# Local attention in a six-layer block: the value products with the preceding tile's keys on two row groups of TensorE

## The chip, the cores and the metric

The kernel is one program on one core of a Trainium2 chip. The metric is the device time of one execution in microseconds, as the median of several. The kernel before took 3763.29 us (three runs, 3762.48 to 3780.51).

## The reference, cut to what matters

The input is `x` of shape (8, 512, 128), in float32. A first stage modulates `x` with six vectors made from `c`, and adds one full attention. Then six layers follow, each a local attention with 16 heads of 64 and a gated feed-forward network. All weights are float32. The change touches the local attention alone:

```python
def local_attention(q, k, v):            # (b, h, n, d), windows of w = 32 tokens
    def look(t):                         # a window sees its own and the preceding one
        p = jnp.pad(t, ((0, 0), (0, 0), (1, 0), (0, 0), (0, 0)))
        return jnp.concatenate([p[:, :, :nw], p[:, :, 1:]], axis=3)
    bk2, bv2 = (look(bk), look(bv))
    sim = jnp.einsum('bhwie,bhwje->bhwij', bq, bk2) * QK_SCALE
    sim = jnp.where(mask, -jnp.finfo(sim.dtype).max, sim)
    attn = jax.nn.softmax(sim, -1)
    out = jnp.einsum('bhwij,bhwje->bhwie', attn, bv2)
```

So each window of 32 queries is multiplied with 64 keys and values: the 32 in front of it and its own 32.

## The kernel before, in words

**Tiles.** A sequence of 512 tokens is cut into four tiles of 128 tokens (`TPB` = 4), j = 0 to 3. A tile has four windows. There are 8 sequences and 6 layers, so 192 tiles, numbered n; four tiles of one sequence in one layer are a batch, and there are 48 batches. All activations stay in the core's memory.

**The pipeline.** Each engine runs an order written out by hand, in slots c = 0, 1, 2, ... (`slot`). A slot handles parts of several tiles: the projections of q and k of tile c, the rotary part of tile c-1 on VectorE, the transposes of q and k (`qk_back`) and the scores of tiles c-2 and c-3, softmax of tile c-3, and the value products (`pv`) and output projection (`out_proj`) of tile c-4. The four kinds of slot (c mod 4 = 0 to 3, "slot 0" to "slot 3" below) differ in what the feed-forward network of an earlier batch puts between. As `pv` lags four tiles, the `pv` of tile j stands in slot j. Four slots are called a turn here.

**What happens in a slot.** ScalarE copies projections to `raw` (`to_raw`, L896), squares them (L904), VectorE sums the squares (L1384), GpSimd takes the power -1/2 (`norms`: L1136, then L1138), VectorE multiplies (`normed`, L1390), VectorE and GpSimd each do half of the rotary part (`cos_part` L1398, `sin_part` L1148, both read `raw`), and VectorE adds the two halves (`rotated`, L1404, which does not read `raw`). `to_raw` of tile n writes the half of `raw` that tile n-2 used, and before it waits until `rotated` of tile n-2 is done. ScalarE's order in a slot is: `to_raw` of two pieces, `qk_to_sbuf`, `to_raw`, squares, `to_raw`, the exponentials (L937), `o_to_sbuf` (L943, the copy of the value products, after `pv`), the second squares, the copies of v, and so on. VectorE's order is: sum of squares, row sums of the exponentials, reciprocal, second sum of squares, `probs` (L1362), `probs_back` (L1377, the transpose of the probabilities in 32x32 blocks into `PTd`), `cos_part`, `rotated`, row maxima (L1340), `less_max`, `normed`.

**The moves.** A window's probabilities stand, after `probs_back`, on the window's own 32 partitions, in `PTd`: half 1 for its own keys, half 0 for the 32 keys in front. `bands` on the queue SP moves them to where the product needs them, by 8 transfers of 32 partitions x 2 KB, each with 16 counts on `band_moved`: the own halves to `PT` (L335), the front halves one window up in `PT` (L338), and the front half of window 0 to partitions 96 to 127 of `BT` (L340), since its keys are the last 32 of the tile in front. SP waits for `probs_back` (L1377), and for the `pv` of the tile before, which frees `PT`.

**The product.** `pv` (L620) waits for all eight, and makes 16 matmuls (one per head) with all 128 keys of the tile: stationary 128x64 of `V`, moving 128x128 of `PT`. Heads u = 0 to 3 of each half go to PSUM bank 2, u = 4 to 7 to bank 5; the even and odd heads go to the lower and upper 64 output partitions. For j > 0, 16 more follow (L627) with the 32 keys in front: stationary 32x64 of `V`, moving 32x32 of `BT`, both on partitions 96 to 127. Each float32 matmul is two instructions in the profile, so L627 has 32 per tile, in 144 tiles.

**Around it in slots 2, 3 and 0.** After `pv` of slot 3, TensorE makes two projections, `qk_back` and `out_proj`; ScalarE copies the result (`attn_to_sbuf`, L952); GpSimd adds it to the running sum (`x_between`, L1157), and only then does its `norms` (L1136, L1138) and `ffn_rstd` (L1175, L1177). ScalarE's `ffn_normed` (L980) and TensorE's `norm_back_ffn` (L658) in slot 0 wait for that.

Of the kernel before, what the change touches and what calls it, by code (L numbers as in the profile page):

```python
# [14 lines left out]
HEADS, DH, W = 16, 64, 32  # L15
INNER = HEADS * DH
HID = int(D * 4 * 2 / 3)
P = 128
TPB = S // P
# [5 lines left out]
HH = HEADS // 2  # L25
# [35 lines left out]
def wait(eng, sem, value):  # L61

    if type(value) is int and value <= 0:
        return
    eng.wait_ge(sem, value)


def adaln_block(nc, x_d, wa_d, ba_d, cT_d, wmod_d,
# [3 lines left out]
    with ctx:  # L72
        def sb(name, shape, dt=F32):
            return ctx.enter_context(nc.sbuf_tensor(name, shape, dt))

        def sem(name):
            return ctx.enter_context(nc.semaphore(name))
# [42 lines left out]
        V = sb("V", [P, 2, INNER])  # L120
        mx = sb("mx", [P, HEADS])
        Pr = sb("Pr", [P, 2 * 512])
        PTd = sb("PTd", [P, 2, HEADS, W])
        PT = sb("PT", [P, NWIN, HEADS, W])
        BT = sb("BT", [P, HEADS, W])
        sm = sb("sm", [P, HEADS])
        rs = sb("rs", [P, HEADS])

# [62 lines left out]
        band_moved = sem("band_moved")  # L191
# [46 lines left out]
        v_out = [sem(f"v_out{c}") for c in range(2)]  # L238
# [5 lines left out]
        cos_ready = sem("cos_ready")  # L244
        sin_ready = sem("sin_ready")
        rot_ready = sem("rot_ready")
# [64 lines left out]
        def layer(n):  # L311
            return n // NT

        @block.sync
        def _(sp):

# [12 lines left out]
            def bands(n, j):  # L329

                sp.wait_ge(pT_ready, n + 1)
                wait(sp, pv_done, n)
                for w in range(NWIN):
                    r = slice(w * W, (w + 1) * W)
                    sp.dma_start(PT[r, w, :, :], PTd[r, 1, :, :]).then_inc(band_moved, 16)  # L335
                    if w > 0:
                        before = slice((w - 1) * W, w * W)
                        sp.dma_start(PT[before, w, :, :], PTd[r, 0, :, :]).then_inc(band_moved, 16)  # L338
                    else:
                        sp.dma_start(BT[P - W:P, :, :], PTd[r, 0, :, :]).then_inc(band_moved, 16)  # L340

            def take_x(b, j):

# [5 lines left out]
            def move(l, m):  # L349
                n = l * NT + m  # L350
                if 0 <= n < NI:
                    bands(n, m % TPB)
# [96 lines left out]
        def _(pe):  # L449
# [162 lines left out]

            def pv(n, b, j):

                pe.wait_ge(band_moved, 128 * n + 128)
                pe.wait_ge(v_out[LAST_VO], n + 1)
                for u in range(HH):
                    for h in range(2):
                        hc = (2 * u + h) * DH
                        mm = nc.tensor.matmul(OUT_BANK[u // 4][h * DH:(h + 1) * DH, (u % 4) * P:(u % 4 + 1) * P],  # L620
                                              V[:, j % 2, hc:hc + DH], PT[:, :, h * HH + u, :],
                                              start=(u % 4 == 0), stop=(j == 0), skip_group_check=True)
                if j > 0:
                    for u in range(HH):
                        for h in range(2):
                            hc = (2 * u + h) * DH
                            mm = nc.tensor.matmul(OUT_BANK[u // 4][h * DH:(h + 1) * DH, (u % 4) * P:(u % 4) * P + W],  # L627
                                                  V[P - W:P, 1 - j % 2, hc:hc + DH], BT[P - W:P, h * HH + u, :],
                                                  start=False, stop=True, skip_group_check=True)
                mm.then_inc(pv_done, 1)  # L630

# [47 lines left out]
            def slot(c):  # L679
                if c % TPB == 0:  # L680
# [17 lines left out]
                    after(c, (2, qkT_out[0]), (3, qkT_out[2]), (5, oT_out))  # L698
                    after(c, (3, qkT_out[3]), (3, qkT_out[1]), (5, oT_out))
                    step(c, 4, pv)  # L700
                    after(c, (0, raw_out[0]), (0, raw_out[1]), (4, v_out[0]))
                    step(c, 3, proj, 4, False, 0)
# [7 lines left out]
                elif c % TPB == 1:  # L710
# [20 lines left out]
                    after(c, (2, qkT_out[0]), (3, qkT_out[2]), (5, oT_out))  # L731
                    after(c, (3, qkT_out[3]), (3, qkT_out[1]), (5, oT_out))
                    step(c, 4, pv)
                    after(c, (0, raw_out[0]), (0, raw_out[1]), (4, v_out[0]))
                    step(c, 3, proj, 4, False, 0)
# [5 lines left out]
                elif c % TPB == 2:  # L741
# [22 lines left out]
                    after(c, (2, qkT_out[0]), (3, qkT_out[2]), (5, oT_out))  # L764
                    after(c, (3, qkT_out[3]), (3, qkT_out[1]), (5, oT_out))
                    step(c, 4, pv)
                    after(c, (0, raw_out[0]), (0, raw_out[1]), (4, v_out[0]))
                    step(c, 3, proj, 4, False, 0)
# [46 lines left out]
        def _(act):  # L815
# [76 lines left out]
            def to_raw(n, b, j, c, first):  # L892
                act.wait_ge(proj_done[c], n + 1)
                if first:
                    wait(act, rot_ready, n - 1)
                nc.scalar.activation(raw[:, j % 2, c * 512:(c + 1) * 512], bank[RAW_BANK[c]][:, :], ACT.Copy)\  # L896
                    .then_inc(raw_out[c], 1)

# [97 lines left out]
            def slot(c):  # L996
                if c % TPB == 0:
                    step(c, 0, to_raw, 1, True)
                    step(c, 0, to_raw, 3, False)
                    step(c, 2, qk_to_sbuf, 0)  # L1000
                    step(c, 0, to_raw, 0, False)
                    step(c, 0, squares, 0)
                    step(c, 0, to_raw, 2, False)
# [201 lines left out]
        def _(dve):  # L1205
# [167 lines left out]
            def probs_back(n, b, j):  # L1373

                dve.wait_ge(prob_ready, n + 1)
                wait(dve, band_moved, 128 * n)
                nc.vector.transpose(PTd[:, :, :, :].rearrange("p t a q -> p a t q"),  # L1377
                                    Pr[:, :].rearrange("p (a t k) -> p a t k", t=2, k=W)).then_inc(pT_ready, 1)

# [41 lines left out]
            def slot(c):  # L1421
                if c % TPB == 0:
# [3 lines left out]
                    step(c, 0, sumsq, 1)  # L1426
                    step(c, 3, probs)
                    step(c, 3, probs_back)
                    step(c, 1, cos_part)
                    step(c, 1, rotated)  # L1430
# [3 lines left out]
                elif c % TPB == 1:  # L1434
# [3 lines left out]
                    step(c, 0, sumsq, 1)  # L1438
                    step(c, 3, probs)
                    step(c, 3, probs_back)  # L1440
                    step(c, 1, cos_part)
                    step(c, 1, rotated)
# [3 lines left out]
                elif c % TPB == 2:  # L1446
                    step(c, 0, sumsq, 0)
                    step(c, 3, sums)
                    step(c, 3, sums_inverse)
                    step(c, 0, sumsq, 1)  # L1450
                    step(c, 3, probs)
                    step(c, 3, probs_back)
                    step(c, 1, cos_part)
                    step(c, 1, rotated)
                    step(c, 2, maxes)
                    step(c, 2, less_max)
                    step(c, 0, normed)
                else:
                    step(c, 0, sumsq, 0)
                    step(c, 3, sums)  # L1460
                    step(c, 3, sums_inverse)
                    step(c, 0, sumsq, 1)
                    step(c, 3, probs)
                    step(c, 3, probs_back)
                    step(c, 1, cos_part)
                    step(c, 1, rotated)
                    batch(c, 1, ffn_stats)
                    step(c, 2, maxes)
                    step(c, 2, less_max)
                    step(c, 0, normed)  # L1470
# [32 lines left out]
```

## Time and profile before

The profiled execution took 3773.0 us, of which the traced span is 3771.0 us.

| | |
|---|---|
| median of three runs | 3763.29 us |
| profiled execution / its span | 3773.0 / 3771.0 us |
| TensorE matmul busy | 3375.2 us (90%) |
| VectorE busy | 3287.8 us (87%) |
| GpSimd busy | 2810.7 us (75%) |
| ScalarE busy | 2435.9 us (65%) |
| transfers' share of 16 DMA engines | 14.5% |
| mean granted TensorE clock | 0.962 of full |

The profile counts an engine as busy when one of its instructions runs; an idle stretch is put down to the instruction elsewhere that ended it. Times in the rows are microseconds from the span's start, unless a row says ns.

### The profile page before, as it was taken

What the parts mean: (1) busy time and instruction counts of PE and PEld (TensorE: products, weight loads), DVE (VectorE), ACT (ScalarE), POOL (GpSimd) and SP (SyncE); (2) the same over time, 40 slices, a digit from 0 to 9 for tenths busy, and PEclk for the clock granted to TensorE, in tenths of its full rate; (3) what the DMA queues carried; (4) which work ended last, traced back from release to release, by engine and by line L of the source; (5) the groups of instructions that cost most, each with busy time, mean ns of one, the idle gap of its engine ahead of it and who ended that gap; (6) DMA issues with size and microseconds to landing.
All of it is one profiled execution on the core that took longest, in us unless ns stands there. A gap on an engine that the chain in (4) does not pass through costs nothing.

```text
span 3771.0 us, 107872 instructions
## 1 busy us (share of the span) xinstructions
PE 3375.2 (90%) x45916; PEld 2204.0 (58%) x46108; DVE 3287.8 (87%) x2914; ACT 2435.9 (65%) x3945; POOL 2810.7 (75%) x1265
## 2 busy tenths in 40 slices
PE   5758999998999999999998999899999999999987
PEld 3325665665665665665666666565666656666664
DVE  6758999998999988999898998898988988998992
ACT  4645766766766766666666676666666666666764
POOL 4457788778787778778777778877777887887771
PEclk9879999999999999999999999999999999999996
DMA  2001111121111111111111111121111111111111
GB/s 72 1 1 36 36 34 38 34 58 41 35 34 39 34 51 44 39 34 35 36 52 44 33 35 35 31 50 44 39 33 34 38 46 45 39 37 35 34 37 36
DMA packets 129694, 141.98 MB, mean 38 GB/s; under 512 B 35388, under 2 KB 73152, under 8 KB 129216
## 3 DMA queue, kind: packets, MB, share of 16 engines
q1 hardware_dynamic: 129216, 135.09, 14.5%
q8 instruction: 364, 5.96, 0.7%
q14 instruction: 114, 0.93, 0.1%
HBM read 19.62 MB, written 2.10 MB: 6 GB/s over the span
## 4 chain that ended last, share of the span: by engine, by line
PE 33%; DVE 23%; POOL 18%; issue 12%; ACT 4%; SPq 3%; DMA 2%; POOLq 0%; ACTq 0%; DVEq 0%
PE bank L570 10%; POOL rr L1138 8%; POOL swp L1148 5%; PE mid L620 4%; DVE Pr L1362 4%; DVE rot L1398 4%; PE mid L579 4%; DVE raw L1390 4%; PE bank L639 4%; PE bank L668 3%; DVE rot L1404 3%; PE mid L607 2%; PE mid L627 2%; DVE ss L1384 2%; PE bank L676 2%
## 5 line engine op out<-in xcount | busy, mean ns | idle before, releaser
L1148 POOL TENSOR_TENSOR swp<-raw,TS 128x1024 f32<-128x1024 f32 x384 | 899.6, 2370 | 622.0 <-DVE raw L1390 622.0
L570 PE MATMUL bank<-wqkv,xs 128*128 128x512 f32 x2304 | 1206.9, 627 | 24.1 <-DMA xs<-F 8.6
L1138 POOL TENSOR_TENSOR rr<-ssm,nhalf 128x32 f32<-128x32 f32 x192 | 1214.8, 6327 | 16.0
L896 ACT ACTIVATE raw<-bank 128x512 f32<-128x512 f32 x768 | 434.6, 592 | 545.0 <-DVE rot L1404 483.8
L579 PEld LDWEIGHTS mid<-ident,rot 128*128 128x128 f32 x3072 | 367.8, 143 | 387.7 <-issue 335.9
L579 PE MATMUL mid<-ident,rot 128*128 128x128 f32 x3072 | 444.6, 278 | 132.7 <-DVE rot L1404 127.3
L1384 DVE TENSOR_REDUCE ss<-sq 128x16 f32<-128x1024 f32 x384 | 463.6, 1207 | 112.1 <-ACT sq L904 111.3
L570 PEld LDWEIGHTS bank<-wqkv,xs 128*128 128x128 f32 x2304 | 387.3, 193 | 289.9 <-issue 194.0
L1390 DVE TENSOR_TENSOR raw<-raw,rr 128x2048 f32<-128x2048 f32 x192 | 469.3, 2444 | 42.6 <-POOL rr L1138 42.6
L1398 DVE TENSOR_TENSOR rot<-raw,TC 128x2048 f32<-128x2048 f32 x192 | 442.2, 2303 | 52.6 <-PE mid L579 51.1
L1404 DVE TENSOR_TENSOR rot<-rot,swp 128x2048 f32<-128x2048 f32 x192 | 440.2, 2292 | 21.0 <-DVE rot L1398 1.4
L620 PEld LDWEIGHTS mid<-PT,V 128*64 128x64 f32 x6144 | 339.6, 138 | 196.2 <-issue 174.2
L904 ACT ACTIVATE sq<-raw 128x1024 f32<-128x1024 f32 x384 | 407.1, 1060 | 29.6 <-DVE ss L1384 22.9
L620 PE MATMUL mid<-PT,V 128*64 128x128 f32 x6144 | 383.6, 278 | 43.3 <-DMA PT<-PTd 40.6
L639 PE MATMUL bank<-OT,fwo 128*128 128x128 f32 x3072 | 387.4, 281 | 1.4 <-ACT OT L943 1.4
L639 PEld LDWEIGHTS bank<-OT,fwo 128*128 128x128 f32 x3072 | 372.5, 198 | 2.0 <-issue 2.0
L1362 DVE TENSOR_TENSOR Pr<-Pr,rs 128x1024 f32<-128x1024 f32 x192 | 351.2, 1829 | 0.1
L607 PEld LDWEIGHTS mid<-kT,qT 64*32 64x32 f32 x24576 | 275.7, 105 | 87.1 <-issue 82.8
L668 PE MATMUL bank<-xn,w 128*128 128x512 f32 (+1 forms) x576 | 313.5, 626 | 6.7 <-ACT ge L993 3.3
L607 PE MATMUL mid<-kT,qT 64*32 64x64 f32 x24576 | 311.1, 226 | 0.7 <-issue 0.7
L921 ACT ACTIVATE qT<-mid 128x512 f32<-128x512 f32 x384 | 229.9, 599 | 103.0 <-PE mid L579 98.7
L943 ACT ACTIVATE OT<-mid 128x512 f32<-128x512 f32 x384 | 208.5, 599 | 112.8 <-PE mid L627 112.7
(132 smaller groups left out, 4340.8 us busy)
## 6 DMA issues: line engine op xcount, KB each, us to landing
PT<-PTd SPq DMA_DIRECT2D x1344, 64.0 KB
xs<-F SPq DMA_DIRECT2D x192, 64.0 KB, 1.9
BT<-PTd SPq DMA_DIRECT2D x192, 64.0 KB
wqkv<-d_wqkv SPq DMA_DIRECT2D x36, 256.0 KB, 2.8
fwo<-d_fwo SPq DMA_DIRECT2D x6, 512.0 KB, 4.3
d_out<-X SPq DMA_DIRECT2D x8, 256.0 KB, 2.3
w<-d_w SPq DMA_DIRECT2D x6, 341.0 KB
w<-d_w SPq DMA_DIRECT2D x6, 128.0 KB
```

The source lines that it names most:

```text
L570: nc.tensor.matmul(bank[bk][:, :], xs[:, j, :], wqkv[:, c, :], start=True, stop=True)\
L579: mm = nc.tensor.transpose(bank[QK_BANK[i]][:, u * P:(u + 1) * P], rot[:, col:col + P], ident[:, :])
L607: mm = nc.tensor.matmul(bank[3 + h][w * W:(w + 1) * W, u * DH:(u + 1) * DH], qT[r, j % 2, u, w * W:(w + 1) * W], kT[r, u, j * P + w * W:j ...
L620: mm = nc.tensor.matmul(OUT_BANK[u // 4][h * DH:(h + 1) * DH, (u % 4) * P:(u % 4 + 1) * P], V[:, j % 2, hc:hc + DH], PT[:, :, h * HH + u, ...
L639: mm = nc.tensor.matmul(bank[6][:, j * P:(j + 1) * P], fwo[:, c, :], OT[:, c, :], start=(c == 0), stop=(c == HH - 1), skip_group_check=True)
L1138: pool.tensor_tensor(rr[:, :], ssm[:, :], nhalf[:, :], ALU.pow).then_inc(rr_ready, 1)
L1148: last = pool.tensor_tensor(dst[:, :, :, t, :], src[:, :, :, 1 - t, :], tab.unsqueeze(2).broadcast_to([P, 2, HEADS, 32]), ALU.mult)
L1362: nc.vector.tensor_tensor(pr, pr, rs[:, :].unsqueeze(2).broadcast_to([P, HEADS, DH]), ALU.mult)\
L1384: nc.vector.tensor_reduce(ss[:, s], sq[:, :].rearrange("p (h d) -> p h d", d=DH), AX.X, ALU.add).then_inc(ss_ready[i], 1)
L1390: nc.vector.tensor_tensor(q, q, rr[:, :].unsqueeze(2).broadcast_to([P, 2 * HEADS, DH]), ALU.mult)\
L1398: nc.vector.tensor_tensor(rot[:, :].rearrange("p (i h d) -> p i h d", i=2, d=DH), q, tab.unsqueeze(2).broadcast_to([P, 2, HEADS, DH]), ALU ...
L1404: nc.vector.tensor_tensor(rot[:, :], rot[:, :], swp[:, :], ALU.add).then_inc(rot_ready, 1)
```

## The change

The 16 products with the keys in front are split by head. For u = 0 to 3 they stay on partitions 96 to 127 and go to bank 2. For u = 4 to 7 both operands are moved to partitions 64 to 95: the probabilities by a transfer of half the size, and the 512 columns of `V` by a transfer into a new buffer `VT`. The products are issued alternately from the two groups. So `bands` has 10 transfers for j > 0 and 7 for j = 0 (whose front half was never read). `moved(n)` counts them. Besides, `to_raw` waits for `sin_part` and `cos_part` of tile n-2 in place of `rotated`.

```diff
+        VT = sb("VT", [P, 512])
+        BT4 = BT[:, :, :].rearrange("p (h u) q -> p h u q", h=2)
+        PTd4 = PTd[:, :, :, :].rearrange("p t (h u) q -> p t h u q", h=2)
...
+        def moved(n):
+
+            return 16 * (37 * (n // TPB) + (0, 7, 17, 27)[n % TPB])
...
                 sp.wait_ge(pT_ready, n + 1)
                 wait(sp, pv_done, n)
+                if j > 0:
+                    sp.wait_ge(v_out[1], n)
+                    sp.dma_start(VT[P - 2 * W:P - W, :], V[P - W:P, 1 - j % 2, 512:1024]).then_inc(band_moved, 16)
                 for w in range(NWIN):
...
-                    else:
-                        sp.dma_start(BT[P - W:P, :, :], PTd[r, 0, :, :]).then_inc(band_moved, 16)
+                    elif j > 0:
+                        for i, rows in enumerate((slice(P - W, P), slice(P - 2 * W, P - W))):
+                            u = slice(4 * i, 4 * i + 4)
+                            sp.dma_start(BT4[rows, :, u, :], PTd4[r, 0, :, u, :]).then_inc(band_moved, 16)
...
-                pe.wait_ge(band_moved, 128 * n + 128)
+                pe.wait_ge(band_moved, moved(n + 1))
...
-                    for u in range(HH):
+                    for u in (0, 4, 1, 5, 2, 6, 3, 7):
                         for h in range(2):
                             hc = (2 * u + h) * DH
                             mm = nc.tensor.matmul(OUT_BANK[u // 4][h * DH:(h + 1) * DH, (u % 4) * P:(u % 4) * P + W],
-                                                  V[P - W:P, 1 - j % 2, hc:hc + DH], BT[P - W:P, h * HH + u, :],
+                                                  V[P - W:P, 1 - j % 2, hc:hc + DH] if u < 4 else VT[P - 2 * W:P - W, hc - 512:hc - 512 + DH],
+                                                  BT[P - W:P, h * HH + u, :] if u < 4 else BT[P - 2 * W:P - W, h * HH + u, :],
                                                   start=False, stop=True, skip_group_check=True)
...
                 if first:
-                    wait(act, rot_ready, n - 1)
+                    wait(act, sin_ready, n - 1)
+                    wait(act, cos_ready, n - 1)
...
-                wait(dve, band_moved, 128 * n)
+                wait(dve, band_moved, moved(n))
```

## Rows read from the trace of the kernel before

**Rows 1.** The page: shares of the chain that ended last, by engine.

```profile
PE 33%; DVE 23%; POOL 18%; issue 12%; ACT 4%; SPq 3%; DMA 2%; POOLq 0%; ACTq 0%; DVEq 0%
```

**Rows 2.** Two turns by windows: length, then busy time (instructions) by engine, granted clock.

```profile
1567.40:1637.50 70.10, 65.77 (x946) 43.51 (x951) 65.24 (x53) 47.88 (x78) 55.12 (x23) 1.00 0.15 36
1995.00:2070.20 75.20, 68.48 (x946) 45.53 (x950) 64.33 (x53) 47.70 (x78) 56.99 (x24) 0.95 0.17 41
```

**Rows 3.** GpSimd in time, slots 3 and 0, a short turn, then a long one.

```profile
1628.47 1.17 POOL L1157 TENSOR_TENSOR FX<-qks,F 128x513 f32<-128x513 f32 x1 [0.86 <-ACT qks L952]
1629.61 0.29 POOL L1136 TENSOR_SCALAR ssm<-ss 128x32 f32<-128x32 f32 x1
1637.54 0.23 POOL L1175 TENSOR_SCALAR vpe<-mv 128x4 f32<-128x4 f32 x1
...
2061.73 1.28 POOL L1157 TENSOR_TENSOR FX<-qks,F 128x513 f32<-128x513 f32 x1 [1.45 <-ACT qks L952]
2062.97 2.34 POOL L1136 TENSOR_SCALAR ssm<-ss 128x32 f32<-128x32 f32 x1
2072.95 2.33 POOL L1175 TENSOR_SCALAR vpe<-mv 128x4 f32<-128x4 f32 x1
```

**Rows 4.** VectorE in time, the same two turns, slot 3.

```profile
1625.29 1.16 DVE L1384 TENSOR_REDUCE ss<-sq 128x16 f32<-128x1024 f32 x1
1629.89 2.25 DVE L1398 TENSOR_TENSOR rot<-raw,TC 128x2048 f32<-128x2048 f32 x1
...
2058.39 1.22 DVE L1384 TENSOR_REDUCE ss<-sq 128x16 f32<-128x1024 f32 x1 [0.34 <-ACT sq L904]
2062.56 2.60 DVE L1398 TENSOR_TENSOR rot<-raw,TC 128x2048 f32<-128x2048 f32 x1
```

**Rows 5.** Groups of instructions by line and shape: busy us, mean ns of one.

```profile
L620 PE MATMUL mid<-PT,V 128*64 128x128 f32 x6144 | 383.6, 278 | 43.3 <-DMA PT<-PTd 40.6 <-issue 1.4
L607 PE MATMUL mid<-kT,qT 64*32 64x64 f32 x24576 | 311.1, 226 | 0.7 <-issue 0.7
L627 PE MATMUL mid<-BT,V 32*64 32x32 f32 x4608 | 162.9, 220 | 0.0
L1175 POOL TENSOR_SCALAR vpe<-mv 128x4 f32<-128x4 f32 x48 | 44.9, 934 | 7.6 <-DVE mv L1415 3.6
```

**Rows 6.** The queue SP in time: start, duration, for slots 1, 2, and 1 (long turn).

```profile
1577.73 0.59 SPq L340 DMA_DIRECT2D BT<-PTd  x1
1578.37 0.58 SPq L335 DMA_DIRECT2D PT<-PTd  x1
...
1598.08 0.60 SPq L338 DMA_DIRECT2D PT<-PTd  x1
...
2012.31 0.59 SPq L338 DMA_DIRECT2D PT<-PTd  x1
```

**Rows 7.** TensorE in time: `pv` of slots 1, 2, 3, 0 (short), and 1 (long).

```profile
1584.93 1.97 PE L620 MATMUL mid<-PT,V 128*64 128x128 f32 x32 [0.49 <-DMA PT<-PTd]
1601.91 1.97 PE L620 MATMUL mid<-PT,V 128*64 128x128 f32 x32
1620.00 1.97 PE L620 MATMUL mid<-PT,V 128*64 128x128 f32 x32 [0.58 <-DMA PT<-PTd]
1637.50 1.97 PE L620 MATMUL mid<-PT,V 128*64 128x128 f32 x32 [0.24 <-DMA PT<-PTd]
...
2018.09 1.97 PE L620 MATMUL mid<-PT,V 128*64 128x128 f32 x32
```

**Rows 8.** The waits: engine and line, whom it waited for, us in total, times.

```profile
ACT raw L896 <- DVE rot L1404: 483.8, 169, 7.0
PEld bank L570 <- ACT raw L896: 57.7, 239, 1.3
```

**Rows 9.** The chain of waits, slot 1 of the short turn.

```profile
1582.63 2.05 DMA PT<-PTd
1586.90 1.05 PE mid L627 x32
```

## Prediction

> **What bounds the kernel now.** I read the page's chain first: no engine carries it alone, TensorE has 33%, VectorE 23%, GpSimd 18%, and SP with its transfers 5% [rows 1]. So the time is set by a ring through four engines, and it has to be read slot by slot. Next I cut the trace into turns of four slots with the windows. They come in two lengths: 70.1 us, and 75.2 us at a granted clock of 0.95 [rows 2]. TensorE's work is the same in both (946 instructions).
>
> What makes a turn long shows in GpSimd's and VectorE's timelines [rows 3, 4]. In the short turn L1157 ends at 1629.64, before VectorE begins `cos_part` at 1629.89; the next GpSimd step takes 0.29 us, and L1175 0.23. In the long turn L1157 ends at 2063.01, after `cos_part` began at 2062.56; the same two steps take 2.34 and 2.33 us. From the end of L1157 to that of L1175 it is 8.1 us in the one and 12.3 in the other, and TensorE's L658 waits behind it. The group of L1175 counts these turns: 48 of mean 0.934 us, made of 0.23 and 2.33, are 16 long ones ((0.934 - 0.23) / 2.10 = 0.335 of 48) [rows 3, 5]. The rows also tell which side came late: in the long turn VectorE waited 0.34 us for the squares that follow slot 3's `pv`, in the short one it did not wait [rows 4]. `pv` late against VectorE makes a long turn. By the Trainium skill, "SBUF — State Buffer", section "SBUF: two separate sides", VectorE and GpSimd share a port pair as an exclusive lock for the whole instruction; the trace's 2.34 in place of 0.29 us agrees.
>
> The other place is `pv` itself. Its idle time is put down to the transfers of `PT`, 40.6 us in all [rows 5]. In the short turn it waits 0.49 us in slot 1, 0.58 in slot 3, 0.24 in slot 0, and not in slot 2 [rows 7]. The chain of slot 1 goes through the last transfer and then `pv` [rows 9]. In the long turn's slot 1, the last transfer is issued at 2012.31 and `pv` starts at 2018.09 [rows 6, 7], so there the transfers have about 3 us to spare (5.8 less a landing of 2.05 [rows 9]).
>
> **The products.** L627 is 32 instructions in 1.05 us [rows 9], 33 ns each, all on one row group; 144 tiles make the 151 us, of which the group shows 162.9 with overlaps [rows 5]. Nothing in the trace shows two row groups of 32. The nearest row is L607, which alternates between two row groups: its 24576 instructions take 311.1 us, 12.7 ns each [rows 5], with twice the moving columns. That end would give 32 x 12.7 = 0.41 us, a gain of 0.64. The other end is no overlap: gain 0; a loss has no mechanism, since instructions and columns stay the same. I take half the time, 0.55 us, nearer to L607: a gain of 0.50 us per tile.
>
> Here a rule speaks against the change: the Trainium skill, "TensorEngine Tiling (Array Packing)", section "Performance Considerations", says that a matmul has some 60 cycles of overhead and that one should not tile what is already small. By it, an estimate from that page, 32 instructions would keep 25 ns each, 0.8 us, a gain of 0.25. L607's 12.7 ns does not agree [rows 5], so the sum goes by the row.
>
> **The transfers.** For j > 0 two are added, for j = 0 one is gone. SP issues one each 0.63 us (1577.73 to 1578.37) [rows 6], and all are queued ahead of the last own half that `pv` waits for. The new ones have 64 KB and twice 32 KB; no row shows a 32 KB one, so each costs between 0.5 and 0.63 us of issue; I take 0.63. So the last of ten lands 1.26 us later in slots 1 to 3, and 0.63 earlier in slot 0. SP's added wait for `v_out` costs nothing: the copy belongs to the slot before. What is queued behind it on SP is the next tile's `xs`, which waits for a later projection anyway.
>
> What is late, slot by slot:
> - Slot 1, short turn: `pv` waits already [rows 7], so it ends 1.26 - 0.50 = 0.76 later. What follows (o_to_sbuf, squares, VectorE) waits for it.
> - Slot 1, long turn: 3 us to spare cover the 1.26; `pv` ends 0.50 earlier.
> - Slot 2: `pv` starts at 1601.91 without a wait, its last transfer was issued at 1598.08 [rows 6, 7]. With a landing of 2.05 and 0.25 to start there is between 0 and 1.5 us to spare; I take 0.7. So it ends 1.26 - 0.7 - 0.50 = 0.06 later: nothing.
> - Slot 3: waits already [rows 7], +0.76.
> - Slot 0: the 0.24 us wait goes, but VectorE's own work and then TensorE carry this slot: 0.
>
> Both waits of a short turn have some turns with a little to spare, so I take 1.3 us for a short turn in place of 1.52, and for a long one -0.50 + 0.76, less the same, 0.2.
>
> **The flips.** TensorE's scores, and with them VectorE's row maxima in slot 3, follow slot 2's `pv` (shift 0.06), while L1157 follows slot 3's `pv` (shift 0.76 against VectorE's transpose). So L1157 moves 0.7 us against `cos_part`. The shown short turn has 1629.89 - 1629.64 = 0.25 us between them [rows 3, 4] and would become long. Others have VectorE further behind, which gives more room. Between 0 and 31 short turns flip; I take 10, each 75.2 - 70.1 = 5.1 us [rows 2]: 51 us.
>
> **The new wait of `to_raw`.** ScalarE waited 483.8 us for `rotated` [rows 8]. Now it may copy some 2.3 us earlier. What comes behind on ScalarE and TensorE is `qk_back`, which needs `rotated` itself, and the third copy needs a projection queued behind `qk_back`. So the wait moves on. What it frees at most is the weight loads' 57.7 us [rows 8], and these lie under running matmuls; I take 0, bounds 0 and 10 us gained.
>
> **The sum.** 21 short turns x 1.3 = 27; 26 long x 0.2 = 5; 10 flips x 5.1 = 51: 83 us. From the profiled execution, 3773.0 + 83 = 3856. That execution is 9.7 us above the median of the runs, so 3846, and I round to 3845.
>
> **The rivals.**
> - *No overlap of row groups* (gain 0). For: L627's two column halves already overlap, and the load of weights may be what takes 33 ns. Against: L607. Then 21 x 2.3 + 26 x 1.2 + 51 = 130 us: 3893. Chance 0.10.
> - *Nearly all turns become long.* For: L1157 moves 0.7 us and the shown margin is 0.25. Against: margins differ by turn. 27 flips x 5.1 = 138, and 43 long x 0.2 + 4 x 1.3 = 14: 3915. Chance 0.13.
> - *Faster: the turns flip back.* One mechanism: slot 3's `pv` is decided by TensorE and not by its transfers. For: over all tiles only 40.6 us are put down to them, 0.2 us a tile [rows 5]. Then slot 3's `pv` comes 0.5 earlier against `cos_part`, and of the 16 long turns 8 become short (-41), with 0.1 us from each turn's products: 3763 - 46 = 3717. It decides where more than 0.8 us (1.26 - 0.50) lie between the last landing and `pv`. Against: the 0.58 us wait of slot 3. Chance 0.20.
> - *It cancels*: added waits and products balance, no turn flips, 3763 +- 19. Chance 0.12.
>
> My forecast has 0.45, with a range of its own from 3800 to 3885 (4 to 18 flips). A difference under 0.5% (19 us) cannot be told from none. So faster 0.20, same 0.12, slower 0.68. The range takes in no overlap and most of "all long", and on the other side half-way into the faster case: 3735 to 3905.
>
> **What would show it.** L627 near 17 ns per instruction (1.05 to 0.55 us a tile); ten SP issues at 0.63 us and `pv`'s idle time for `PT` well above 40.6 us; mean of L1175 at 0.934 + 10 x 2.10 / 48 = 1.37 us; ScalarE's wait for `rotated` gone and found again as one for `qk_back` or the projection. I am wrong if L1175's mean falls below 0.93, or if `pv` of slot 3 does not wait.

## The result and the profile after

The changed kernel takes 3898.4 us (median of four runs, 3865.59 to 3915.31) against 3766.91 before: a ratio of 1.033, with a 95% interval of 1.026 to 1.041. It is slower by 131 us. I had forecast 3845 and slower, with a range of its own from 3800 to 3885; the result lies 13 us above that one, and inside the whole range of 3735 to 3905. Its profiled execution took 3891.65 us, of which the span is 3889.2.

The chain of the page, by engine. GpSimd has become first, and SP with its transfers has gone from 5% to 14%, against [rows 1]:

```profile
POOL 28%; PE 18%; DVE 15%; issue 14%; SPq 10%; ACT 5%; DMA 4%; POOLq 0%; ACTq 0%; DVEq 0%
```

Two turns by windows, with the columns of [rows 2]. There still are the two lengths, 70.8 and 75.2 us:

```profile
2284.30:2355.10 70.80, 64.39 (x950) 41.79 (x950) 65.40 (x53) 47.90 (x78) 55.65 (x24) 1.00 0.15 37
1769.30:1844.50 75.20, 65.99 (x951) 43.33 (x950) 64.59 (x53) 48.15 (x78) 57.14 (x24) 0.95 0.15 35
```

The groups that answer to [rows 5] (L632 is `pv`, L639 the products with the keys in front, L1189 the former L1175):

```profile
L632 PE MATMUL mid<-PT,V 128*64 128x128 f32 x6144 | 391.0, 281 | 142.1 <-DMA PT<-PTd 141.2
...
L639 PE MATMUL mid<-BT,VT 32*64 32x32 f32 x2304 | 96.4, 223 | 0.0
L639 PE MATMUL mid<-BT,V 32*64 32x32 f32 x2304 | 96.4, 223 | 0.0
...
L1189 POOL TENSOR_SCALAR vpe<-mv 128x4 f32<-128x4 f32 x48 | 78.4, 1634 | 7.6 <-DVE mv L1429 3.6
```

`pv` waits 141.2 us for transfers, before 40.6. L1189's mean is 1.634 us, so (1.634 - 0.23) / 2.10 x 48 = 32 turns are long, before 16.

The chain in slot 1 of the short turn, from SP's first issue to VectorE's next step, answers to [rows 6, 9]:

```profile
2294.63 0.51 SPq L342
...
2295.19 0.58 SPq L345
...
2301.31 2.04 DMA PT<-PTd
...
2303.60 1.97 PE mid L632 x32
2305.57 0.64 PE mid L639 x32
```

Ten issues take 6.68 us to the start of the last, which lands 2.04 later; then `pv` runs, and the block of L639 takes 0.64 us (0.60 in the middle one of the 144 tiles, 1.05 before). TensorE in that turn, slots 1, 2 and 3, answers to [rows 7]. Slot 2 waits too now, and over all tiles most: of the 142.1 us in front of `pv`, 59.8 stand in slot 2 (1.1 before), 37.8 in slot 1 (11.8 before), 43.0 in slot 3 (22.3 before) and 1.6 in slot 0 (8.1 before).

```profile
2303.60 1.97 PE L632 MATMUL mid<-PT,V 128*64 128x128 f32 x32 [1.94 <-DMA PT<-PTd]
...
2320.51 1.97 PE L632 MATMUL mid<-PT,V 128*64 128x128 f32 x32 [0.52 <-DMA PT<-PTd]
...
2338.00 1.97 PE L632 MATMUL mid<-PT,V 128*64 128x128 f32 x32 [0.43 <-DMA PT<-PTd]
```

GpSimd, then VectorE, at the end of slot 3 in the long turn, answer to [rows 3, 4]. VectorE waited 0.93 us for the squares behind `pv`, and began `cos_part` at 1836.95, before L1171 (the former L1157) ended at 1837.60; the next GpSimd step took 2.33 us:

```profile
1836.33 1.27 POOL L1171 TENSOR_TENSOR FX<-qks,F 128x513 f32<-128x513 f32 x1 [2.03 <-ACT qks L966]
1837.57 2.33 POOL L1150 TENSOR_SCALAR ssm<-ss 128x32 f32<-128x32 f32 x1
```

```profile
1833.01 1.22 DVE L1398 TENSOR_REDUCE ss<-sq 128x16 f32<-128x1024 f32 x1 [0.93 <-ACT sq L918]
...
1836.95 2.79 DVE L1412 TENSOR_TENSOR rot<-raw,TC 128x2048 f32<-128x2048 f32 x1 [0.29 <-PE mid L591]
```

The waits that answer to [rows 8]. ScalarE's wait is now for `cos_part`, and the rest of it stands at the next copy, which needs `qk_back`:

```profile
ACT qT L935 <- PE mid L591: 365.8, 315, 5.2
...
ACT raw L910 <- DVE rot L1412: 168.3, 98, 4.7
```

I timed each turn from one start of slot 0's `pv` to the next, and called it long if the L1175 in it took over 1.2 us. In a long turn that instruction comes some 3 us after the turn's start. It stands behind the meeting of GpSimd and VectorE in slot 3 of the turn in front, so the meeting at the end of one turn makes the next one long. So the rows of slot 3 at 2062 in [rows 3, 4] belong to the turn that starts at 2070.21 and takes 76.38 us, and those at 1630 to the one that starts at 1637.50 and takes 70.65. In both cases the two neighbouring turns are of one kind, and so it is for the long turn shown after, so the readings hold. The 47 turns between give the whole difference:

| | long turns: mean | short turns: mean | sum |
|---|---|---|---|
| before | 16: 75.26 us | 31: 70.01 us | 3374 us |
| after | 32: 75.48 us | 15: 71.69 us | 3491 us |

16 turns have gone from short to long, 16 x 5.25 = 84 us; the 15 short ones are 1.68 longer, 25 us; the 32 long ones 0.22 longer, 7 us. Together 116 of the 118 us between the spans. The very first turn after counts as short with 74.46 us, 13.7 of them at half clock; without the first turns the short ones are 1.47 longer.

A long turn holds more than GpSimd's slow steps. TensorE stands still near its start, and the granted clock falls to its lower level (1.2 GHz) before that wait ends. In the long turn of [rows 2] it is 0.50 from 2001.5 to 2008.3 and 1.00 in the rest. TensorE's L658 and L639, first in the short turn and then in the long one:

```profile
1570.42 0.63 PE L658 MATMUL bank<-ident,xn 128*128 128x128 f32 x4
...
1572.18 1.95 PE L639 MATMUL bank<-OT,fwo 128*128 128x128 f32 x16
...
2002.27 1.09 PE L658 MATMUL bank<-ident,xn 128*128 128x128 f32 x4 [4.25 <-ACT xn L980]
...
2005.71 3.19 PE L639 MATMUL bank<-OT,fwo 128*128 128x128 f32 x16
```

TensorE waits 4.25 us until 2002.27, and then the same 16 instructions take 3.19 us in place of 1.95; over the turn it is busy 68.48 us in place of 65.77 [rows 2]. All 16 long turns before and all 32 after have such a stretch at half clock: 7.0 and 6.8 us a turn on average, against 0.5 and 1.6 us in the short ones. So the 5.25 us are a wait and a slower TensorE behind it; no run parts the two.

### The profile page after: what moved, and what is told of

The parts are those of the page before. It is cut to its first block, busy times and chain, and to the rows that moved or that the text cites. A ratio compares the mean times of both kernels' runs of the same rounds, so it can differ in the third digit from the quotient of the medians.

```text
span 3889.2 us, 108304 instructions
## 1 busy us (share of the span) xinstructions
PE 3341.7 (86%) x46108; PEld 2169.6 (56%) x46108; DVE 3258.3 (84%) x2914; ACT 2444.1 (63%) x3945; POOL 2808.0 (72%) x1265
## 4 chain that ended last, share of the span: by engine, by line
POOL 28%; PE 18%; DVE 15%; issue 14%; SPq 10%; ACT 5%; DMA 4%; POOLq 0%; ACTq 0%; DVEq 0%
POOL rr L1152 12%; POOL swp L1162 6%; PE bank L582 5%; SPq L345 5%; DVE Pr L1376 4%; DMA PT<-PTd 4%; PE mid L632 4%; POOL ssm L1150 3%; SPq L348 2%; DVE raw L1404 2%; SPq L352 2%; DVE PTd L1391 2%; POOL vpe L1189 2%; PE bank L681 2%; PE mid L591 2%
## 5 line engine op out<-in xcount | busy, mean ns | idle before, releaser
L1152 POOL TENSOR_TENSOR rr<-ssm,nhalf 128x32 f32<-128x32 f32 x192 | 1161.0, 6047 | 16.0
L591 PEld LDWEIGHTS mid<-ident,rot 128*128 128x128 f32 x3072 | 374.0, 145 | 384.3 <-issue 335.1
L591 PE MATMUL mid<-ident,rot 128*128 128x128 f32 x3072 | 452.0, 281 | 117.3 <-DVE rot L1418 111.0
L632 PE MATMUL mid<-PT,V 128*64 128x128 f32 x6144 | 391.0, 281 | 142.1 <-DMA PT<-PTd 141.2
L632 PEld LDWEIGHTS mid<-PT,V 128*64 128x64 f32 x6144 | 347.3, 140 | 293.2 <-issue 293.2
L1404 DVE TENSOR_TENSOR raw<-raw,rr 128x2048 f32<-128x2048 f32 x192 | 445.0, 2318 | 71.0 <-POOL rr L1152 71.0
L652 PEld LDWEIGHTS bank<-OT,fwo 128*128 128x128 f32 x3072 | 381.3, 202 | 2.0 <-issue 2.0
L1376 DVE TENSOR_TENSOR Pr<-Pr,rs 128x1024 f32<-128x1024 f32 x192 | 336.5, 1753 | 0.1
```

Of the source, the lines that this page charges most:

```text
L591: mm = nc.tensor.transpose(bank[QK_BANK[i]][:, u * P:(u + 1) * P], rot[:, col:col + P], ident[:, :])
L652: mm = nc.tensor.matmul(bank[6][:, j * P:(j + 1) * P], fwo[:, c, :], OT[:, c, :], start=(c == 0), stop=(c == HH - 1), skip_group_check=True)
L1152: pool.tensor_tensor(rr[:, :], ssm[:, :], nhalf[:, :], ALU.pow).then_inc(rr_ready, 1)
L1376: nc.vector.tensor_tensor(pr, pr, rs[:, :].unsqueeze(2).broadcast_to([P, HEADS, DH]), ALU.mult)\
L1404: nc.vector.tensor_tensor(q, q, rr[:, :].unsqueeze(2).broadcast_to([P, 2 * HEADS, DH]), ALU.mult)\
```

## The experiments

Twelve kernels were run. "Long" is from the mean of L1175 or its like (0.23 and 2.33 us), "short turn" is the mean timed as above. "Held" means with the wait that e4 adds, so that no turn can become long. e2, e3 and e12 leave half of the products with the keys in front out of the result.

| kernel | median us | ratio to before, interval | long | short turn us |
|---|---|---|---|---|
| e1 new wait of `to_raw` alone | 3762.6 | 1.000 (0.996 to 1.004) | 17 | 69.80 |
| e2 products alone | 3673.6 | 0.977 (0.972 to 0.982) | 2 | 69.52 |
| e3 transfers alone | 3945.8 | 1.049 (1.045 to 1.053) | 44 | 71.85 |
| e4 before, held | 3708.1 | 0.986 (0.982 to 0.990) | 0 | 70.57 |
| e5 after, held | 3790.1 | 1.007 (1.005 to 1.009) | 0 | 72.12 |
| e6 after, V's transfer early | 3730.9 | 0.991 (0.988 to 0.994) | 12 | 70.17 |
| e7 before, two queues | 3819.0 | 1.016 (1.011 to 1.021) | 7 | 72.32 |
| e8 all, two queues, held | 3896.2 | 1.036 (1.032 to 1.040) | 0 | 74.58 |
| e9 e6, held | 3717.5 | 0.986 (0.981 to 0.991) | 0 | 70.56 |
| e10 e9, queue shared for j = 1, 3 | 3672.4 | 0.974 (0.968 to 0.980) | 0 | 69.81 |
| e11 before, shared like e10, held | 3689.4 | 0.978 (0.974 to 0.982) | 0 | 70.14 |
| e12 e3, held | 3814.8 | 1.012 (1.008 to 1.016) | 0 | 72.85 |

**The three parts of the change.** e1 has only the new wait:

```diff
-                    wait(act, rot_ready, n - 1)
+                    wait(act, sin_ready, n - 1)
+                    wait(act, cos_ready, n - 1)
```

> The kernel before, with only the new wait of to_raw (for sin_part and cos_part of tile n-2 in place of rotated). My theory (the two added transfers delay pv, and pv's delay makes more turns long): 0, between -10 and +10 us, and 16 long turns as before (L1175 mean 0.93 us). Rival A (the early copies on ScalarE shift the ring and cause the loss): +60 us or more, with L1175's mean well above 0.93.

It came out at 0 (the interval is 14 us to either side), so rival A falls: the new wait costs nothing by itself. ScalarE's wait only moved, as in the rows above: 191.6 us are left at the first copy, and 306.3 stand at `qT`, where the kernel before had 98.7.

e2 has the product's loop of the change, on an otherwise unchanged kernel:

```diff
+                pool.memset(BT[:, :, :], 0.0)
+                pool.memset(VT[:, :], 0.0)
...
-                    for u in range(HH):
+                    for u in (0, 4, 1, 5, 2, 6, 3, 7):
```

> The kernel before, with the 16 products on two row groups but without any added transfer: VT and the lower group's rows of BT hold zeros, so half of the products with the keys in front are left out of the result. My theory: the block takes 0.60 us in place of 1.05 as in the changed kernel; of a turn's three blocks two stand on the path, so 47 x 2 x 0.45 = 42 us faster, 3725, and about as many long turns as before, since slot 2's and slot 3's pv both come earlier. Rival B (switching between row groups costs TensorE elsewhere what it saves here, and is part of the loss): 0 or slower.

It gained twice as much, 87 us. Rival B falls: the products speed the kernel up. What I had missed is that the products also decide between the lengths of turn: only 2 were left long (14 x 5.25 = 74 us), while the short turn gained 0.49 us, 22 us over 45 turns. The two make 96 us, of the 98 between the spans of the two profiled executions.

e3 is the change without its product's loop and without the new wait:

```diff
-                    for u in (0, 4, 1, 5, 2, 6, 3, 7):
+                    for u in range(HH):
...
-                                                  V[P - W:P, 1 - j % 2, hc:hc + DH] if u < 4 else VT[P - 2 * W:P - W, hc - 512:hc - 512 + DH],
-                                                  BT[P - W:P, h * HH + u, :] if u < 4 else BT[P - 2 * W:P - W, h * HH + u, :],
+                                                  V[P - W:P, 1 - j % 2, hc:hc + DH], BT[P - W:P, h * HH + u, :],
```

> The kernel before, with the changed kernel's transfers (10 for j > 0, 7 for j = 0, among them V's and the lower group's) but all products on the one row group as before; the products of u = 4 to 7 read rows that hold zeros. My theory: slower than the changed kernel by what e2 gains: 3767 + 131 + 42 = 3940 us, L1175's mean near 1.6 us (32 long turns), pv waiting for PT some 140 us. Rival A and rival B: the loss is elsewhere, so under 3830.

3946 against 3940 expected, so the transfers are the loss. The time was hit partly by luck: 44 turns were long where I had put 32.

**The long turns.** e4 adds one wait to the kernel before, in `cos_part`:

```diff
                 dve.wait_ge(qn_ready, n + 1)
+                if j == 2 and n + 1 < NI:
+                    dve.wait_ge(ssm_ready, n + 2)
```

> The kernel before, with one wait added: in slot 3, cos_part on VectorE waits until GpSimd has done its L1136 of the next tile, so that GpSimd always gets in first. It takes the long turns away and nothing else. My theory (a turn is long because cos_part starts before GpSimd's step): L1175's mean 0.23 us, no long turn, 16 x 5.1 = 82 us less, of which VectorE's new wait (up to 0.7 us in those 16 turns) gives back 10: 3695 us. Rival C (the long turns' 5 us are due to something else that comes together with the order, such as the TensorE clock, and VectorE's wait only adds): 3767 or slower.

Slot 3 of one of its turns, GpSimd and then VectorE:

```profile
2042.53 1.28 POOL L1157 TENSOR_TENSOR FX<-qks,F 128x513 f32<-128x513 f32 x1 [1.21 <-ACT qks L952]
2043.78 0.29 POOL L1136 TENSOR_SCALAR ssm<-ss 128x32 f32<-128x32 f32 x1
2044.15 5.46 POOL L1138 TENSOR_TENSOR rr<-ssm,nhalf 128x32 f32<-128x32 f32 x1
```

```profile
2044.15 2.39 DVE L1400 TENSOR_TENSOR rot<-raw,TC 128x2048 f32<-128x2048 f32 x1 [0.48 <-POOL ssm L1136]
```

VectorE waits 0.48 us here, GpSimd's step takes 0.29 and its power 5.46 us. No turn is long, and 52 us are gained: a kernel with one more wait is faster. Rival C falls as it was put: the added wait changes only when `cos_part` starts, and the long turns are gone, so that order makes them. What follows from the order went with them, TensorE's wait for L980 (76.7 us in all before, 11.2 in e4) and part of the time at half clock (2.7 us a turn over all turns before, 1.8 in e4). My "and nothing else" was wrong: the power of slot 3 is no longer behind `cos_part` and takes 5.46 us in place of 7.48 in nearly all turns, not only in the 16.

The gain is 30 us under the 82 that 16 long turns seemed to cost, because the held turn has 70.57 us and not 70.01. The clock goes with this difference: 15 of the held turns have no stretch at half clock and take 70.02 us on average, 14 have one of about 3.4 us and take 71.71. Whether it is the cause was not tried.

e5, e12 and e9 put the same wait into the changed kernel, into e3 and into e6.

> The changed kernel with e4's wait (cos_part in slot 3 behind GpSimd's L1136), so that no turn can become long. My theory (the loss has two parts: pv's delay on the path, and the turns that become long): L1175's mean 0.23 us; the 32 long turns' 4 us each go (e4 gave 52 to 64 us for 16), so 3898 - 130 = 3768, that is 60 us over e4's 3708, which is the plain delay: two waits a turn, each +1.5 us of landing less 0.45 of product less some slack, 1.3 us a turn. Rival D (the long turns are a by-product of lateness and the loss is all plain delay): it stays within 30 us of 3898.

> e3 (all transfers of the change, products on one row group) with e4's wait. It splits e3's 186 us into plain delay and long turns; with e4, e5 and e3 it makes the square. My theory: no long turn, the plain delay of e5 (82 us over e4) plus the product's part, 40: 3708 + 82 + 40 = 3830 us. If nearly all of e3's loss were long turns: 3740 or less.

With e4 they make the split without long turns: the transfers cost e12 - e4 = 107 us (2.3 a turn), the products give back e12 - e5 = 25 (0.5 a turn), so 82 us of plain delay. The rest, (e5 to after, 108 us) less (e4 to before, 52), is 56 us of more long turns. The two add up to after less before by construction; they make 138 and not 131 because the kernel before took 3760 us beside e4 and 3767 in the first comparison. The medians of the kernel before moved by 11 us from one round of runs to another, so each part is known to some 10 us. By the held turns of the table the parts are 107, 34 and 73 us. e5 came 22 us over my expectation, e12 15 under.

**How many transfers stand on the way.** e6 takes V's transfer out from behind the wait for the probabilities, and gives it a double buffer and a semaphore for that:

```diff
+                if j > 0:
+                    sp.wait_ge(v_out[1], n)
+                    wait(sp, pv_done, n - 1)
+                    sp.dma_start(VT[P - 2 * W:P - W, j % 2, :], V[P - W:P, 1 - j % 2, 512:1024]).then_inc(vt_moved, 16)
                 sp.wait_ge(pT_ready, n + 1)
                 wait(sp, pv_done, n)
-                if j > 0:
-                    ...
```

> The changed kernel, but V's transfer is issued before SP waits for the probabilities, into a double buffer with its own semaphore, so only 9 transfers stand between probs_back and pv, not 10. My theory: one issue of 0.63 us less on the way; between before and after, about half: L1175's mean near 1.3 us, 3830 us, pv's wait for PT between 45 and 140 us. Rival E (the row-group products or the half-sized transfers with 512-byte pieces are what costs, not the count of issues): 3880 or more.

It was better than expected by 100 us, and 0.9% faster than the kernel before. With the products on two row groups, 8, 9 and 10 transfers behind `probs_back` give 3674 (e2), 3731 (e6) and 3898 us (after), with 2, 12 and 32 long turns. The first step costs 57 us, the second 167. Time from the transpose's end to the last landing, for j = 3, is 7.3, 8.1 and 8.7 us in the middle. Rival E falls: e6 has the products, the half-sized transfers and the bytes of the changed kernel, so they are not what costs the 167 us. The step of 57 us is less clean: e6 has V's transfer and the two half-sized ones, e2 neither.

e9 is e6 with e4's wait.

> e6 (9 transfers on the way, V's ahead) with e4's wait. My theory: e6 has 12 long turns (L1175's mean 0.76 us), each worth about 4 us by e4: 3731 - 48 = 3683 us, L1175's mean 0.23, faster than before and than the changed kernel. Rival: with few long turns the wait gives nothing back and costs VectorE, 3731 or more.

Only 14 us came of it, and 3717 in place of 3683: with 12 long turns there is less to win, and the held turn has 70.56 us in place of 70.17. Against e5, V's transfer ahead is worth 73 us here, 1.56 a turn. So of the 167 us between e6 and after, 94 came with the long turns. But e9 is no better than e4: on SP alone, with no turn long, the change's idea earns nothing.

**Two queues.** e7 gives half of the kernel before's transfers (two of eight for j = 2) to ScalarE's queue. The place in slot 0 is shown; the other slots have theirs:

```diff
+            def moves(n, b, j):
+                act.wait_ge(pT_ready, n + 1)
+                wait(act, pv_done, n)
+                for dst, src in shares(j)[1]:
+                    nc.scalar.dma_start(dst, src).then_inc(band_moved, 16)
...
                     step(c, 2, qk_to_sbuf, 3)
+                    step(c, 3, moves)
                     batch(c, 2, lin_to_sbuf, 1)
```

> The kernel before, with its 8 transfers shared between two queues: 4 stay on SP, 4 are issued by ScalarE at the end of its slot (in slot 1, where it is busy, 2 after the first gelu). No products changed. My theory (what pv waits for is SP's serial issue of 0.63 us each): the last landing comes some 1.5 to 2.5 us earlier, pv's wait for PT falls from 40 to under 15 us, slot 3's pv comes earlier against cos_part, fewer than 5 long turns, 3690 us, less what ScalarE's 0.6 us per issue costs. Rival F (it is the transfers' bandwidth or landing, not the issue): pv waits as before, 3767 or more.

> All together: row-group products, V's transfer early, the other 9 (7) shared between SP and ScalarE, and e4's wait. My theory: TensorE and VectorE carry the ring, pv waits for nothing, no long turn, the product's 0.45 us counts in two slots of a turn: e4's 3708 less 40 for the product and less 20 for the landing: 3650 us, faster than before and than e2's 3674. Rival F: 3740 or more.

Both went the wrong way, though the transfers did what was wanted: in e7 the last landing for j = 1 is 4.2 us behind the transpose and not 7.3, and `pv` waits 3 us in all; 7 turns were long, where I had put under 5. Rival F's time came without its condition, a `pv` that waits as before, so it falls too. The loss is ScalarE's. In slot 0 of e7, its queue issues while TensorE waits for the copy L981 behind it; ScalarE and TensorE in time:

```profile
2051.34 1.80 ACTq L898 DMA_DIRECT2D PT<-PTd  x3
2053.17 0.61 ACTq L898 DMA_DIRECT2D BT<-PTd  x1
...
2053.89 0.69 ACT L981 ACTIVATE wmod<-bank,b 128x512 f32<-128x512 f32 x1 [1.96 <-issue]
...
2054.63 1.13 PE L669 MATMUL bank<-xn,w 128*128 128x512 f32 x2 [1.67 <-ACT wmod L981]
```

e10 moves that issue behind the copy, and shares only for j = 1 and 3, three transfers each:

```diff
                     step(c, 2, qk_to_sbuf, 3)
-                    step(c, 3, moves)
                     batch(c, 2, lin_to_sbuf, 1)
+                    step(c, 3, moves)
```

> e9, and for tiles j = 1 and 3 three of the nine transfers are issued by ScalarE, where its order leaves room (behind the copy of the linear part in slot 0, ahead of ffn_to_sbuf in slot 2); none in slots 1 and 3. In e7 and e8 ScalarE's issues in slot 0 held up a copy that TensorE waits for. My theory: pv of slots 1 and 3 waits no more, 3683 less up to 25: 3660 us. If ScalarE's 0.6 us per issue cost the ring wherever they stand: over 3700.

TensorE waits for this copy 133.0 us in all in e7 and 148.4 in e8, and 1.6 in e10, as in the kernel before. With 3672 us, 12 over my expectation, e10 is the fastest kernel that computes the whole result (e2, with half of the products with the keys in front left out, took 3674). Between e8 and e10 lie 224 us for the place and number of ScalarE's issues; how much each of the two has was not tried. e11 does the same to the kernel before, with the products on one row group:

> The kernel before (products on one row group, 8 transfers, the wait of to_raw as before) with e4's wait and e10's sharing of the queue: three transfers issued by ScalarE for j = 1 and 3. It tells what the change's own idea is worth once its transfers are out of the way. My theory: the product's 0.45 us still stands on the path twice a turn, so e11 is slower than e10 by 20 to 42 us: 3700 us. Rival: the products are hidden and the sharing alone makes e10 fast: within 8 us of 3672.

It is 17 us slower than e10. The intervals of the two ratios overlap, but the held turns say the same, 70.14 against 69.81 us. So the change as a whole, products, V's transfer ahead, one more transfer and the new wait of `to_raw` together, is worth some 17 us in this setting, less than the 20 to 42 that I expected; the ratios alone do not rule out none.

## Why the prediction was right in sign, and what was mis-sized

- *What bounds the kernel.* Right. The last landing as the wait of `pv` (e6 shortens it, e7 takes it away) and the two lengths of turn (e4) were confirmed. That four engines form a ring is read from the chain, and no run tests it.
- *The products.* 0.55 us was forecast for the block, 0.60 to 0.64 measured, 19 to 20 ns an instruction. The gain of 0.41 to 0.45 a block comes to about 0.5 us a turn on the path (0.5 from e2's short turn, 0.7 from the held turns of e12 and e5), not 2 x 0.50: mis-sized. The 25 ns an instruction that I had worked out, as an estimate, from the Trainium skill, "TensorEngine Tiling (Array Packing)", section "Performance Considerations", was too high here; L639's 19 ns lies between it and L607's 12.7.
- *The transfers.* +1.26 us was forecast for the last landing; 1.1 to 1.5 came, for j = 1 from 7.3 to 8.8, for j = 2 from 7.4 to 8.7, for j = 3 from 7.6 to 8.7 in the middle. Right in size, with some luck: the time from the first issue to the last grew by 1.9 us, from 4.4 to 6.3 in the middle, more than two issues. The term "between 0.5 and 0.63 us" for a 32 KB transfer was a little low: from its issue to the next it is 0.68 us in the middle, against 0.63 for 64 KB. By the Trainium skill, "DMA: Bandwidth & Descriptors", section "🎯 Rules for kernel authors", spreading transfers over queues does not raise bandwidth but saves issue time; e7's 4.2 in place of 7.3 us agrees, and it was the issue time that counted.
- *Per turn.* 1.3 us for a short turn, measured 1.68 (1.47 without the first turn); 0.2 for a long one, measured 0.22; 5.1 for a flip, measured 5.25. The 0.2 was hit partly by luck, since slot 2's `pv`, put at no wait, waits 1.52 us on average in the long turns.
- *The flips.* This term was mis-sized most: "Between 0 and 31 short turns flip; I take 10". It was 16, and 84 us in place of 51. The turn shown for it was also one off, as said above. The sum by the measured count would have been 15 x 1.3 + 32 x 0.2 + 16 x 5.1 = 108 us, against 118 between the spans.
- *Slot 2.* "So it ends 0.06 later: nothing" was wrong: its `pv` waits 0.52 us in the turn above, 1.3 in the middle turn. Over all tiles it has the largest part of `pv`'s wait, 59.8 us. The 0.7 us to spare was taken from the middle of a wide bound.
- *The wait of `to_raw`.* Right, 0 (e1).
- *The rivals.* "It cancels" and "faster" fell with the result. What "faster" described does happen where no transfer is added: e2 turned 14 long turns short. "No overlap" named 3893 us, which is nearest to the measured time, but that is chance: the block went from 1.05 to 0.60 us. "All long" was the near one: e3, with 44 of 48, shows where that ends.

Why more turns flipped is only partly shown. In slot 2 of a turn there is a second meeting of GpSimd and VectorE. Before, GpSimd's power L1138 there was slow (over 7 us, not 5.46) in 38 of 48 turns, and then its next sum (L1169, at 1619.41) overlapped VectorE's `normed`, which took 3.09 us in place of 2.28. Rows of the short turn from before, and of the long one after:

```profile
1611.83 2.29 DVE L1398 TENSOR_TENSOR rot<-raw,TC 128x2048 f32<-128x2048 f32 x1
1612.03 7.41 POOL L1138 TENSOR_TENSOR rr<-ssm,nhalf 128x32 f32<-128x32 f32 x1
...
1619.74 3.09 DVE L1390 TENSOR_TENSOR raw<-raw,rr 128x2048 f32<-128x2048 f32 x1
```

```profile
1819.32 5.46 POOL L1152 TENSOR_TENSOR rr<-ssm,nhalf 128x32 f32<-128x32 f32 x1
1819.56 2.29 DVE L1412 TENSOR_TENSOR rot<-raw,TC 128x2048 f32<-128x2048 f32 x1 [0.62 <-PE mid L591]
...
1827.26 2.28 DVE L1404 TENSOR_TENSOR raw<-raw,rr 128x2048 f32<-128x2048 f32 x1
```

After, it was slow in 9 turns. In the turn shown, TensorE's L591, which comes behind the late `pv` of slot 2, holds up `cos_part` by 0.62 us, so the power starts first. VectorE's `normed` is then 0.8 us shorter, VectorE comes earlier to slot 3, and its `cos_part` starts before GpSimd's L1171 (before: L1157) has ended. By this reading the slow power had kept turns short. The single turns agree: in the kernel before, 8 of the 37 turns with a slow power in slot 2 lost the meeting of slot 3 (made the next turn long), and 8 of the 10 with a fast one; after, 3 of 8 and 29 of 39; in e7, 0 of 40 and 7 of 7. The totals of e2 (41 slow, 2 long) and e3 (6 slow, 44 long) go the same way. But no run changed slot 2's meeting by itself, and a late `pv` may lie behind both, so this cause stays argued.

## What to carry to other kernels

Before adding a transfer for a faster product, look at what stands between the data's last writer and the product: here one transfer more behind the wait of a serial queue (V's, e6 against the changed kernel) cost 167 us, 94 of them with the long turns, while with the same transfer issued before the wait the kernel was 0.9% faster than before. With no long turns on one queue (e9 against e4) the change won nothing. Where turns of one loop have two lengths, find the instruction pair whose order decides, count how often each way occurs, and predict the count, not only the mean shift. Holding one of the two back with a wait can be faster than letting both run. And look at the granted clock of such a turn: part of its length can stand behind the wait, in a slower TensorE.

## What the runs showed of the hardware

- A GpSimd instruction of 0.29 us takes 2.33 when VectorE's 2.3 us `cos_part` has begun before it; one of 5.46 (the power) takes 7.3 to 7.5 when it starts behind `cos_part`. A wait of 0.5 us on VectorE in slot 3 removes both there (e4).
- A block of 32 float32 instructions with 32 moving columns takes 0.60 us (19 ns each) when it alternates between two row groups of 32, and 1.05 us (33 ns each) on one.
- While TensorE waited 4.25 us (1998.0 to 2002.3 in the kernel before), the granted clock fell to 0.50; it stayed there for 6.8 us, and 16 matmul instructions took 3.19 us in place of 1.95. Every long turn of the kernels before and after has a stretch at half clock.
- An issue on ScalarE's queue holds ScalarE's own next instruction for some 0.6 us each, 2.4 us for four (e7), and SP's time from one issue to the next is 0.63 us for 64 KB and 0.68 for 32 KB in the middle.
